# Order of work at the start of the last batch of a pooled-attention kernel: a bank moved, a tile split and convolved in another place

## What is computed

```python
qk  = relu(bn(conv1x1(x, qk_w)))            # 256 channels
val = relu(bn(conv1x1(x, v_w)))             # 512 channels
key, value = psp(qk), psp(val)              # max over the cells of 1x1, 3x3, 6x6, 8x8 grids: 110 cells
scores = softmax(einsum('bnc,bcs->bns', query(qk), key) * 256 ** -0.5)
y = einsum('bns,bsc->bnc', scores, value)
out = x + bn(conv1x1(y, out_w))             # 512 channels
```

## Time and profile before

| | us |
|---|---|
| median of 3 runs | 1323.11 (1322.58 to 1323.71) |
| the profiled execution | 1325.19 |
| its span, first to last instruction | 1323.5 |
| PE busy in it | 1287.3 (97%) |
| mean granted clock of TensorE | 0.993 of full |

### The profile page before, as it was taken

One profiled execution on the slowest core, in us unless ns is written; L12 is line 12 of the kernel. 1 busy time (PEld: TensorE's weight loads), 2 busy tenths in 40 slices (PEclk: granted clock), 3 DMA queues, 4 the chain that ended last, 5 costly groups with the idle time before them and its releaser, 6 DMA issues.

```text
span 1323.5 us, 16789 instructions
## 1 busy us (share of the span) xinstructions
PE 1287.3 (97%) x5539; PEld 1039.0 (79%) x5539; DVE 949.4 (72%) x2171; ACT 688.9 (52%) x1017; POOL 953.2 (72%) x414
## 2 busy tenths in 40 slices
PE   7999999999999999999999999999999998999996
PEld 6777788887888878887888878888788876888875
DVE  6555677777777768778777777777787776876466
ACT  4333555644555654455654456565545555754421
POOL 1888988877888867787777787887688645665522
PEclk9999999999999999999999999999999998999998
DMA  6323356566676656667566667666666768995226
GB/s 219 116 96 112 111 172 214 198 212 222 207 238 229 209 168 230 230 222 229 194 199 220 228 206 236 217 204 201 208 214 230 241 238 300 304 308 199 96 96 255
DMA packets 134537, 272.20 MB, mean 206 GB/s; under 512 B 9226, under 2 KB 9266, under 8 KB 134450
## 3 DMA queue, kind: packets, MB, share of 16 engines
q1 hardware_dynamic: 133874, 270.07, 60.5%
q10 hardware_dynamic: 576, 1.05, 0.2%
HBM read 174.61 MB, written 96.47 MB: 205 GB/s over the span
## 4 chain that ended last, share of the span: by engine, by line
PE 78%; DVE 7%; POOL 7%; ACT 3%; DMA 3%; issue 2%; SPq 0%; DVEq 0%; ACTq 0%; POOLq 0%
PE conv_ps L689 16%; PE conv_ps L687 16%; PE conv_ps L691 16%; POOL xl L578 5%; PE out_ps L773 4%; PE out_ps L774 4%; PE out_ps L775 4%; PE conv_ps L672 3%; PE conv_ps L673 3%; PE conv_ps L671 3%; DMA xa<-x 2%; PE score_ps L744 2%; PE score_ps L745 2%; PE score_ps L743 2%; DVE row_max L1319 1%
## 5 line engine op out<-in xcount | busy, mean ns | idle before, releaser
L1319 DVE TENSOR_REDUCE row_max<-conv_ps 128x64 f32<-128x384 f32 (+2 forms) x576 | 284.6, 530 | 152.0 <-ACT q_out L1029 68.2
L578 POOL TENSOR_TENSOR xl<-xa,xh 128x1024 fp32r<-128x1024 f32 x108 | 257.8, 2409 | 83.1 <-ACT xh L958 83.1
L687 PE MATMUL conv_ps<-xh,sh 128*128 128x512 f32 x648 | 253.5, 391 | 4.4 <-POOL xl L578 2.4
L689 PE MATMUL conv_ps<-xh,sl 128*128 128x512 f32 x648 | 254.4, 393 | 0.0
L691 PE MATMUL conv_ps<-xl,sh 128*128 128x512 f32 x648 | 254.1, 392 | 0.0
L578 POOL TENSOR_TENSOR xl<-tt,xh 128x1024 fp32r<-128x1024 f32 x81 | 193.8, 2407 | 10.1 <-ACT xh L958 10.1
L687 PE MATMUL conv_ps<-xh,wh 128*128 128x512 f32 x486 | 190.2, 391 | 4.8 <-POOL xl L578 2.7
L691 PE MATMUL conv_ps<-xl,wh 128*128 128x512 f32 x486 | 190.7, 392 | 0.0
L689 PE MATMUL conv_ps<-xh,wl 128*128 128x512 f32 x486 | 190.7, 392 | 0.0
L1459 DVE SCALAR_TENSOR_TENSOR xo<-out_ps,shift,xo 128x512 f32<-128x512 f32 x205 | 152.0, 745 | 42.2 <-DMA xo<-x 24.4
L966 ACT ACTIVATE conv_ps<-conv_ps 128x512 f32<-128x512 f32 x81 | 47.2, 583 | 254.1 <-PE conv_ps L691 253.4
(11 more groups left out here) (227 smaller groups left out, 2537.2 us busy)
## 6 DMA issues: line engine op xcount, KB each, us to landing
xa<-x SPq DMA_DIRECT2D x148, 512.0 KB, 5.5
xo<-x SPq DMA_DIRECT2D x104, 512.0 KB, 4.3
out<-xo SPq DMA_DIRECT2D x104, 512.0 KB, 3.7
queries<-q_out SPq DMA_DIRECT2D x112, 256.0 KB, 2.5
q_in<-queries SPq DMA_DIRECT2D x50, 512.0 KB, 4.0
tt<-x SPq DMA_DIRECT2D x13, 512.0 KB, 5.1
out<-tt SPq DMA_DIRECT2D x13, 512.0 KB, 3.9
early<-queries SPq DMA_DIRECT2D x6, 512.0 KB, 7.4
```

Of the source, the lines that this page charges most:

```text
L578: nc.gpsimd.tensor_tensor(xl[:, b0:b1, :], raw, xh[:, b0:b1, :], ALU.subtract).then_inc(x_lo, 1)
L687: nc.tensor.matmul(out[:, :], hi[:, k, :], xh[:, b + k, :], start=first, stop=False, skip_group_check=True)
L689: nc.tensor.matmul(out[:, :], lo[:, k, :], xh[:, b + k, :], start=False, stop=False, skip_group_check=True)
L1319: last = nc.vector.tensor_reduce(row_max[:, c, n, :], src[:, r0_ * W:r1_ * W].rearrange("p (r w) -> p w r", w=W), AX.X, ALU.max)
```

## The change

The values of image 6 are turned in `conv_ps[3]`. `scores(49)`, which uses that bank, now waits for `values_lo(6)`, and `sums(48)` no longer does. The turning waits for the pooled rows of image 6 instead of the last reciprocal.

PE: at s = 56 `conv(56, 4)` comes in front of project(46, 2) and (46, 3), `conv(56, 5)` behind them. At s = 57 sums(48) comes in front of `conv(57, 5)`, and `conv(58, 4)`, which was at s = 58, stands between scores(49) and project(48, 0).

ACT: `split_hi(57, 1)` moves up in front of `split_p_hi(47)`, both `store_q(56, ...)` in front of `finish_keys`; the two `split_hi(58, ...)` move from s = 57 to behind `finish_values`, in front of `store_q(57, 0)`, `exps(48)`, `split_q_hi(49)` and `values_hi(6)`. At s = 57 the order is guess(48), store_q(57, 1), split_p_hi(48), exps(49), split_q_hi(50), store_q(58, 0).

POOL: `split_lo(58, 0)` and `(58, 1)` come in front of `split_q_lo(49)` instead of behind `split_q_lo(50)`.

DVE: at s = 56 `refine(47)`, `normalise(47)`, the two add_outs and `split_p_lo(47)` come in front of the pooling of cells and both `finish_grids`; `keys_lo` comes behind the rows of tile 56 and `cell_values_lo` behind `add_out(47, 0)` and `(47, 1)`. At s = 57 refine(48), normalise(48) and split_p_lo(48) come first, and `pool_tile_rows(58, 4)` moves there from s = 58.

SP's order is the same. No instruction is added or taken away.

```diff
         def pv_bank(k):
-            return sum_ps if k == B - 2 else out_ps[1]
+            return conv_ps[3] if k == B - 2 else out_ps[1]
...
             for s in range(LAST, X):
                 if LAST < s < S:
                     split_q_lo(s - (NT - 1))
-                if s + 1 < X:
-                    split_lo(s + 1, 0)
-                    split_lo(s + 1, 1)
+                for n in (s + 1, s + 2) if s == LAST else () if s == LAST + 1 else (s + 1,):
+                    if n < X:
+                        split_lo(n, 0)
+                        split_lo(n, 1)
...
                 if a == LAST - NT + 1:
-                    pe.wait_ge(rows_pooled, CC * LAST)
+                    pe.wait_ge(vo_lo, B - 1)
...
                 wait(pe, rsum_ready, a)
-                if a == LAST - NT:
-                    pe.wait_ge(vo_lo, B - 1)
...
                     pe.wait_ge(value_ready, k + 1)
-                    wait(pe, rsum_ready if k == B - 2 else out_added, (1 if k == B - 2 else OC) * NT * k)
+                    if k == B - 2:
+                        pe.wait_ge(rows_pooled, CC * LAST)
+                    else:
+                        wait(pe, out_added, OC * NT * k)
...
             for s in range(LAST, S):
                 ap, ac = s - NT - 1, s - NT
+                sums(ap)
                 if s == LAST + 1:
                     conv(s, 5)
-                sums(ap)
                 if s == LAST:
+                    conv(s, 4)
                     projections((ap - 1, 2), (ap - 1, 3))
-                    conv(s, 4)
                     conv(s, 5)
...
                 scores(ac)
-                if s > LAST + 1:
+                if s == LAST + 1:
+                    conv(s + 1, 4)
+                else:
                     project(ap - 1, 2)
                     project(ap - 1, 3)
-                    conv(s, 4)
+                    if s > LAST + 2:
+                        conv(s, 4)
                     conv(s, 5)
...
             for s in range(LAST, X):
                 ap, ac = s - NT - 1, s - NT
+                if 0 <= ap < S - 2:
+                    guess(ap)
                 if s == LAST + 1:
                     store_q(s, 1)
-                if 0 <= ap < S - 2:
-                    guess(ap)
+                    split_p_hi(ap)
+                    exps(ac)
+                    split_q_hi(ac + 1)
+                    store_q(s + 1, 0)
+                    continue
...
                     split_hi(s + 1, 0)
+                if s == LAST:
+                    split_hi(s + 1, 1)
                 if 0 <= ap < S - 2:
                     split_p_hi(ap)
-                if s in (LAST, S):
-                    finish_keys(ac // NT)
-                if s + 1 < X:
-                    split_hi(s + 1, 1)
                 if s == LAST:
                     store_q(s, 0)
                     store_q(s, 1)
+                if s in (LAST, S):
+                    finish_keys(ac // NT)
+                if LAST < s < X - 1:
+                    split_hi(s + 1, 1)
+                if s == LAST:
                     finish_values(ac // NT)
+                    split_hi(s + 2, 0)
+                    split_hi(s + 2, 1)
                     store_q(s + 1, 0)
...
                 if s == LAST:
                     add_out(ap - 1, 1)
-                    pool_cells(NT - 2, VC, CC, CC * LAST)
-                    pool_cells(NT - 1, VC, CC, CC * LAST)
-                if s == LAST:
-                    finish_grids(VC, CC, keys_pooled)
-                if s > LAST + 1 or s == LAST:
-                    refine(ap)
-                    normalise(ap)
+                refine(ap)
+                normalise(ap)
                 if s == LAST:
                     add_out(ap - 1, 2)
                     add_out(ap - 1, 3)
                     split_p_lo(ap)
+                    pool_cells(NT - 2, VC, CC, CC * LAST)
+                    pool_cells(NT - 1, VC, CC, CC * LAST)
+                    finish_grids(VC, CC, keys_pooled)
                     finish_grids(0, VC, values_pooled)
-                    keys_lo(ac // NT)
                     pool_tile_rows(s, 4)
                     pool_tile_rows(s, 5)
-                    cell_values_lo(ac // NT)
+                    keys_lo(ac // NT)
                     add_out(ap, 0)
                     add_out(ap, 1)
+                    cell_values_lo(ac // NT)
...
                 if s == LAST + 1:
+                    split_p_lo(ap)
                     pool_tile_rows(s, 5)
-                    refine(ap)
-                    normalise(ap)
+                    split_e_lo(ac)
+                    pool_tile_cells(s, VC, CC)
+                    add_out(ap, 0)
+                    add_out(ap, 1)
+                    pool_tile_rows(s + 1, 4)
+                    continue
```

More of the change, by code:

```diff
@@ L1211, in _ @@
                 if LAST + 1 < s < S:
-                    store_q(s, 0)
+                    if s > LAST + 2:
+                        store_q(s, 0)
                     store_q(s, 1)
@@ L1618, in _ @@
                 if s == LAST + 1:
+                    split_p_lo(ap)
                     pool_tile_rows(s, 5)
-                    refine(ap)
-                    normalise(ap)
+                    split_e_lo(ac)
[4 more added lines that the diff above has]
+                    continue
                 split_e_lo(ac)
-                if s > LAST + 1:
-                    add_out(ap - 1, 2)
+                add_out(ap - 1, 2)
                 split_p_lo(ap)
-                if s > LAST + 1:
-                    add_out(ap - 1, 3)
+                add_out(ap - 1, 3)
+                if s > LAST + 2:
                     pool_tile_cells(s - 1, VC, CC)
                     pool_tile_rows(s, 4)
-                    pool_tile_rows(s, 5)
+                pool_tile_rows(s, 5)
                 add_out(ap, 0)
```

## The result

The changed kernel takes 1316.07 us in the median (1314.11 to 1316.77, 4 runs), the kernel before 1323.41 (1322.58 to 1325.10, 4 runs). The ratio is 0.9943 with a 95% interval of 0.9931 to 0.9956: by the ratio 7.5 us less, between 5.8 and 9.1, a little over half a per cent. The forecast was 1314.9, with 1312.0 to 1318.0.

The account below looks back on a forecast made before the run. PE, busy for 97% of the span, was taken as the bound. 9.9 us lost less 1.6 of waits left gave 8.3, taken as 8.2, off 1323.11: 1314.9 us, range 1312.0 to 1318.0.

Parts of the forecast that it names:

- The knot and its price: PE, sums(47) to sums(51): 9.9 us lost: 4.6 long pause at project(48, 0), 2.5 clock, 2.8 short waits.
- the wait of 0.4: PE's wait for add_out(46, 1) near 1080.8 us; conv(56, 4) moved forward fills it.
- the 1.0 for POOL: PE's wait of 1.0 us for POOL's half of tile 57; goes, as ACT splits that tile earlier.
- Reading of the short waits: PE waits seen in 1080 to 1180 us: 4.4, 1.0 and two of 0.8 together, then seven steps without one.
- The waits left: PE waits kept: 0.6 at project(47, 2), 0.1 at sums(48), 0.4 at scores(50), 0.5 at project(49, 0); 1.6 us.
- the bank: Values turned in conv_ps3: costs nothing by itself, since scores(49) needs it over 1.5 us after values_lo(6).
- conv(58, 4) as cover: PE runs conv(58, 4) before project(48, 0), hiding the old 6.42 us chain from sums(48) by 1.0.
- Rival 1: DVE and POOL exclude each other near cell_values_lo: turning 1.0 us later, split_e_lo(48) 0.5 more; 1316.4 us; chance 0.12.
- Rival 2: DMA queues, near full around the stretch, become the bound: 1316.9 us, or 1319.3 with only 3.8 saved; chance 0.10.
- Rival 3: Clock in the last stage: 14 low-clock matmuls, 2.7 us, spared by the shift: 1312.2 us; chance 0.09.
- Rivals 4 and 5: ACT delays sums(48), half kept, 1319.0 us, chance 0.05; ACT stalls on tile 58's late load, 1326 or more, chance 0.04.
- The signs: What would confirm: sums(51) about 1125 (wrong before 1123 or after 1129), no PE wait over 1 us, clock 1.00.

Follow-up runs that it names:

- experiment 4: The changed kernel with conv(58, 4), its store and its rows back at s = 58, tile 58 still split early: median 1317.95 us, ratio 0.9956.
- experiment 2: The kernel before with values turned in conv_ps3 and sums(48), guess, refine and normalise earlier: sums(47) to sums(51) 53.07 us against 52.88.
- experiment 7: The changed kernel with the values turned in sum_ps again and sums(48) behind conv(57, 5): sums(47) to sums(51) 47.55 us against 45.18.
- experiment 8: The changed kernel with both split_hi(58) in front of finish_values on ACT: sums(47) to sums(51) 47.66 us.
- experiment 9: The changed kernel with tile 58's load issued behind that of residual 96: sums(47) to sums(51) 52.73 us.

## Why the prediction was right, and where its steps were off

- *The knot and its price.* "4.6 in the long pause, 2.5 to the clock" and 2.8 in the short waits, 9.9 in all. The pause, the low clock and the wait of 0.4 are gone in the changed kernel's trace, and of the 1.0 for POOL 0.1 is left; 7.70 of the forecast 8.2 came. In the stretch the prediction's time for sums(48), 17.8 after sums(47), was met with 17.88.
- *Reading of the short waits.* The prediction took the view's 0.8 for xo as two waits of this stretch, with seven steps without a wait behind it. One of the two, 0.31, lies at 1174.52, over 40 us behind the stretch, and is in both kernels. The 2.8 was right as a remainder all the same: PE's timeline has four holds in the stretch, 2.6 together with the longer spacing behind each, and 0.2 is spacing elsewhere.
- *The waits left,* forecast 0.6, 0.1, 0.4 and 0.5, from the distances in the trace above each less one spacing of 0.23: 0.46 at project(47, 2), 0.10 at sums(48), 0.27 at scores(50), 0.43 at project(49, 0). That is 1.26 in place of 1.6, all four in their places.
- *The mis-sized terms* are small. Behind each of the four waits the next matmul follows after 0.34 instead of 0.23 (1090.27 to 1090.61 above), 0.4 in all, so the waits with their edges are 1.7, and conv(57, 4) has a hold of 0.1 for POOL. The other spacings average 0.2307 in place of a steady step's 0.229, 0.3 over 188 matmuls; why is open. Together these are the 0.5 between 8.2 and 7.7. Only about 0.3 of the "9.9 lost" was never there to be won.
- *The edits at s = 56,* which the prediction did not price as a group: the table's first column falls from 19.66 with the bank alone to 17.88 in the changed kernel and in the one without cover, so conv(56, 4) forward, the early split of tile 57 and DVE's new order bring 1.8 us together. What each brings was not tried.
- *conv(58, 4) as cover.* The reason given was incomplete. The prediction had the old chain of 6.42 hidden "by 1.0" by it. In the trace the chain from sums(48) to the end of p_lo(48) takes 5.6, since split_p_hi(48) now stands first on ACT (before, DVE stood idle 0.85 for it); the cover hides it by 1.9, and without the cover only 0.76 shows (experiment 4). The larger part of the cover's 2.1 us comes from the way of the queries from scores(49) to scores(50). The prediction had this way only as the 0.4 at scores(50), with the cover in place.
- *The bank* "costs nothing by itself" was right. That it brings nothing by itself either (experiment 2), and 2.4 us with ACT's new order (experiment 7), the prediction did not say. Nor did it say that the other edits bring 5.3 us without it.
- *Rival 1* did not come: DVE was first by 0.9, forecast 0.8. Forced (experiment 8), it costs 2.5 us of stretch; by the expectation 0.6 of that is the later value chain alone, which leaves 1.9, where the prediction had 1.5.
- *Rival 2* did not come; 1 MB more was still carried without a wait of PE.
- *Rival 3* was seen in part: 8 low-clock matmuls in the last stage in place of 13, 1.16 us of the profiled execution. It can't be credited to the change: the table has 0, 6, 7, 8, 13 and 14 for the same last stage with the same waits of PE.
- *Rivals 4 and 5* did not come; the price of 5 was mis-sized, as said at experiment 9.
- *The signs.* sums(51) is at 1123.32, just inside the 1123 to 1129 that the prediction allowed, since this execution was 2.24 early before the stretch; counted from the old start of sums(47), 1080.38, it would be 1125.56. project(48, 0) has no wait. That the median came within 1.2 us of the forecast is partly luck: the medians of the changed kernel, 1316.07 and 1314.47, differ by more than that between two sets of runs.

## What to carry to other kernels

A dependency that is taken away moves the end only if each engine on the way passes the result on: look for what stands in front of the next instruction of the chain on its own engine, and change that order with it. (The new order alone, in the kernel before, was not run here; with the early tile 58, but without the bank, it kept 5.3 of 7.7 us.) When one chain's pause is removed, list the other chains that ran hidden in it (here the split of the queries) and lay them out against the new, shorter step. Compare by a stretch between two fixed instructions when the start and the last stage vary by more than the change is worth.

## What the runs showed that I had not expected

- The fall of the clock inside the stretch does not follow from the waits near it alone. With waits of 0.78 and 1.79 the clock fell for 7 matmuls in the kernel with the bank and p first, and with 0.76 and 1.79, or 0.77 and 1.66, it did not fall in the kernels of experiments 4 and 7. The first of these also keeps the old waits of 0.4 and 1.0 earlier in the stretch, which the other two have not. It fell behind each pause of 4.4 and 5.3 us. What sets it in between is open.
- The last stage, the same instructions in all of these kernels, lasted 65.58 us with no matmul at the low clock, 67.1 with 8 and 68.3 with 13 or 14: up to 2.8 us of a comparison of totals can be this. PE's distances of over 0.7 us from one matmul to the next are the same to 0.01 us in the kernel before, the changed kernel and the one with two more DMAs (1.0, 0.7, 1.4, 1.2 and 2.5 us, in this order from 29.5 us after sums(61)). In the first the clock fell right behind the last of them, in the second 1 us later, in the third not at all. So PE's work up to there does not decide it; what does is open.
- In the kernel with two more DMAs of 512 KB the queues' busy share was 1.01 to 1.07 from 1105 to 1120, and nothing came late that PE waited for. The share of busy time alone is no sign that transfers bound the time.
